# Splitting K into its two fp16 halves on POOL from an fp32 copy, and ACT's projection copy between a slot's two exponentials

## The chip, the cores and the metric

One core of a Trainium2 chip runs the whole kernel in one launch. The engines that matter are PE (TensorE, matrix products), ACT (ScalarE), DVE (VectorE), POOL (GpSimd) and SP (SyncE), which here only issues transfers. The metric is the device time of one execution in microseconds (us).

## The reference, cut to what matters

Four transformer-like layers run over `x` of 16 batches x 56 tokens x 128 features. Layers 1, 2 and 3 each hold a cross-attention over the same context `ctx`, 16 x 1500 x 128, with 16 heads of 8 features:

```
h   = (ctx - mean) / sqrt(var + eps)          # layers 1 and 2 (layer 1 scales and shifts it too); layer 3 uses ctx as it is
k   = h @ Wk + bk ;  v = h @ Wv + bv          # 1500 x 128 each, per batch
att = softmax(q @ k.T / sqrt(8))              # 56 x 1500 per head
x   = x + (att @ v) @ Wo + bo
```

Layer 0 is one attention over `ctx` with a mixture of three experts behind it; layers 2 and 3 also have a self-attention over 56 tokens ahead of the cross-attention and a feed-forward block behind it. All is fp32 in the reference. The kernel forms `q @ k.T` from fp16 halves: k_hi is k rounded to fp16 and k_lo = k - k_hi, again in fp16; q is treated likewise, and the products hi·hi, hi·lo and lo·hi are summed in one matrix product over 50 rows.

## The kernel before, in words

Every engine has its own instruction stream, written out by hand, and the streams meet through semaphores (`wait_ge` on one, `then_inc` to another). An engine executes its stream strictly in order, so a wait holds back all that stands behind it.

A cross-attention (`cross`, once per layer 1, 2 and 3) is a software pipeline over 16 batches, `pipeline`: `attend(batch, following, behind, third)` works on batch b, on b+1 (`following`), b+2 (`behind`) and b+3 (`third`) at once. One attend is cut into 12 slots c, each for 125 context rows. In slot c, PE computes the scores of b (`scores`, 8 products into two halves, L1153), then two or three `unit` products of b+1 (L1101), whose maximum DVE takes (L1552), in odd slots the products of probabilities and v of two earlier slots (`values`, L1127), and last one `misc` step. ACT takes the two exponentials of the slot (L795), one for each half of the scores. PE's scores of slot c+1 wait for the first exponential of slot c, so for little else.

The misc steps prepare context for later batches. There are nine for a batch (`MISC`): T0, T1, T2 transpose the context (L1011), K0, K1, K2 form k (L1016, 500 context rows each), V0, V1, V2 form v (L1022). `SLOT_MISC` places them: V2 of b+1 in slot 0; T0, T1, T2, K0 of b+2 in slots 1 to 4; K1, K2 in 6 and 8; V0, V1 in 9 and 10. They all use one PSUM bank, so that a misc product must wait until the one before has been copied out. ACT copies it out (`misc` in ACT's part: T at L717 or L720, K at L725, V at L729) at the start of the next slot, ahead of that slot's exponentials. For a K step, ACT writes k_hi (fp16) and DVE then reads the bank again and k_hi, and writes k_lo (L1460, `k_low`); PE's next misc product waits for both (L1000, L1001). On DVE `k_low` stands behind the maxima of the slot. Before the pipeline of a layer starts, the misc steps of batches 0 and 1 run beside the expert network of layer 0 or beside the self-attention (`ahead`).

SP moves k on: `k_out` (L407) writes the two halves of a third of k to DRAM, `k_in` (L419) reads it back in six pieces so that the heads lie as the matrix products need them. It waits for `k_lo_done` and for the transfers before it. In one attend SP issues k_out 0, k_in 0, k_out 1, k_in 1, k_out 2 for b+2, and then `load` (L373): the context of b+4, 750 KB, into one of two buffers. The third k_in of that batch comes at the start of the next attend.

POOL normalises the context of b+3 (`normalise`, 12 instructions at L585) in layers 1 and 2, once it has been loaded; in layer 3 it does nothing in the pipeline. In the self-attention POOL copies operands for each of the 16 batches (`self_copies`, L544 to L548). The ring of probabilities has RING = 6 slots.

## Time and profile before

| | |
|---|---|
| median of 3 runs | 2066.11 us (2053.47 to 2067.04) |
| the profiled execution | 2056.51 us, span of its instructions 2054.7 us |
| mean granted TensorE clock | 0.892 of full speed |
| busy share of the span | PE 80%, DVE 60%, ACT 49%, POOL 21% |

The profile is of one execution. PE's share is a modelled one, since its products are pipelined. In a timeline, a row gives the start (us from the span's start), the duration, engine, line, operation, output and input with shapes, the number of instructions merged, and in square brackets the idle time of the engine just before it with what ended it. "issue" there means that the profile shows nothing that was waited for. "SPq" is the issue of a transfer on SP; its duration is that of the issue and not of the transfer. The cross-attentions lie at about 410 to 800 us (layer 1), 1005 to 1410 us (layer 2) and 1610 to 2010 us (layer 3).

### The profile page before, as it was taken

The page shows a single profiled execution, that of the slowest core. Times are in us where ns is not written, and L with a number is a line of the kernel's source. Part 1 is how long each engine was busy: PE and PEld are TensorE (multiplying, and loading weights), DVE is VectorE, ACT ScalarE, POOL GpSimd, SP SyncE. Part 2 cuts the span into 40 slices and gives each one's busy share as a digit, 9 for nine tenths or more (in the row PEclk, how much of TensorE's full clock was granted, in tenths as well). Part 3 has the DMA queues.
Part 4 walks back from the last instruction along what each step waited for, and adds up shares of the span by engine and source line. Part 5 has one row for each costly group of instructions (what it writes and reads, how often), then busy time and mean ns, then how long its engine had stood idle before and what let it go on. Part 6 is the DMA issues. An engine that isn't in the chain of part 4 may idle for free.

```text
span 2054.7 us, 53923 instructions
## 1 busy us (share of the span) xinstructions
PE 1635.4 (80%) x20495; PEld 1030.7 (50%) x20495; DVE 1236.0 (60%) x2433; ACT 1004.1 (49%) x1911; POOL 422.9 (21%) x611
## 2 busy tenths in 40 slices
PE   4788777588887887787688888887785888888876
PEld 3465544255555555443355555555342455555554
DVE  5454443567775776364677777773364777777762
ACT  1243322166665666242366666663242466666662
POOL 7000133013331333135033333310131000000000
PEclk9798988599998998796699999996796799999997
DMA  5021122234443442040344444430040444444410
GB/s 174 26 77 64 45 44 62 55 82 112 112 110 94 113 102 73 1 103 3 72 112 113 111 109 111 110 98 14 0 102 11 92 116 117 114 114 112 106 43 9
DMA packets 178537, 166.32 MB, mean 81 GB/s; under 512 B 67551, under 2 KB 168098, under 8 KB 178402
## 3 DMA queue, kind: packets, MB, share of 16 engines
q1 hardware_dynamic: 176818, 163.35, 30.2%
q8 instruction: 97, 1.59, 0.4%
q10 hardware_dynamic: 1008, 1.05, 0.2%
q14 instruction: 38, 0.31, 0.0%
q0 software_dynamic: 576, 0.02, 0.0%
HBM read 114.46 MB, written 40.08 MB: 75 GB/s over the span
## 4 chain that ended last, share of the span: by engine, by line
PE 64%; issue 13%; DVE 10%; ACT 10%; DMA 1%; POOL 1%; ACTq 0%; DVEq 0%; SPq 0%; POOLq 0%
PE PS L1127 11%; PE PS L1022 8%; PE PS L1153 8%; PE PS L1016 8%; PE PS L862 6%; PE PS L1101 5%; PE PS L1011 3%; PE PS L941 3%; ACT q_parts L795 2%; DVE mx L1552 2%; PE PS L1227 2%; PE PS L959 2%; ACT v_sb L729 2%; ACT cxT L720 2%; PE PS L932 1%
## 5 line engine op out<-in xcount | busy, mean ns | idle before, releaser
L1552 DVE TENSOR_REDUCE mx<-PS 112x1 f32<-112x500 f32 x1152 | 718.4, 671 | 295.8 <-PE PS L1101 291.5
L795 ACT ACTIVATE q_parts<-PS 125x448 f32<-125x448 f32 x1152 | 562.2, 544 | 108.8 <-PE PS L1153 105.0
L585 POOL TENSOR_SCALAR cx<-cx,norm_b 125x128 f32<-125x128 f32 x384 | 303.5, 813 | 590.7 <-DMA cx<-in_ctx 488.2
L1153 PE MATMUL PS<-q_st,k_st 50*125 50x112 f16 x4608 | 263.1, 236 | 40.1 <-ACT q_parts L795 23.2
L1153 PEld LDWEIGHTS PS<-q_st,k_st 50*125 50x125 f16 x4608 | 186.4, 140 | 213.7 <-ACT q_parts L795 121.7
L1101 PE MATMUL PS<-k_st,q_mx 50*112 50x500 f16 x1152 | 262.5, 403 | 38.8 <-issue 24.2
L1127 PE MATMUL PS<-q_parts,v_sb 125*18 125x112 f32 x9216 | 291.4, 270 | 0.0
L1127 PEld LDWEIGHTS PS<-q_parts,v_sb 125*18 125x18 f32 x9216 | 218.4, 101 | 60.7 <-issue 52.1
L729 ACT ACTIVATE v_sb<-PS 125x512 f32<-125x512 f32 x144 | 87.1, 605 | 186.7 <-PE PS L1022 186.6
L725 ACT ACTIVATE k_hi<-PS,vec 128x500 f16<-128x500 f32 x144 | 97.5, 677 | 129.0 <-PE PS L1016 129.0
L1101 PEld LDWEIGHTS PS<-k_st,q_mx 50*112 50x112 f16 x1152 | 91.5, 133 | 74.5 <-issue 44.9
L1460 DVE SCALAR_TENSOR_TENSOR k_lo<-PS,vec,k_hi 128x500 f16<-128x500 f32 x144 | 104.8, 728 | 20.0 <-ACT k_hi L725 20.0
L1011 PE MATMUL PS<-ident,cx 125*128 125x125 f32 x576 | 97.1, 293 | 22.6 <-ACT cxT L717 11.8
L1011 PEld LDWEIGHTS PS<-ident,cx 125*128 125x128 f32 x576 | 62.6, 146 | 63.4 <-issue 26.3
L1022 PE MATMUL PS<-L_xcond_Wkv,cxT 128*125 128x128 f32 x384 | 61.1, 308 | 27.3 <-issue 22.6
L1022 PE MATMUL PS<-L_xcond_W_kvc,cxT 128*125 128x128 f32 x384 | 61.1, 308 | 25.0 <-issue 22.9
L1016 PE MATMUL PS<-cxT,L_xcond_Wkv 128*128 128x500 f32 x96 | 54.7, 653 | 30.8 <-issue 25.9
L813 ACT ACTIVATE A<-A 56x896 f32<-56x896 f32 x32 | 30.4, 949 | 92.4 <-DVE A L1661 92.4
L1022 PE MATMUL PS<-L_xcond_ca_vw,cxT 128*125 128x128 f32 x384 | 55.2, 287 | 25.3 <-issue 22.9
L782 ACT ACTIVATE q_st<-PS 2x448 f16<-2x448 f32 x48 | 25.7, 535 | 101.4 <-PE PS L1112 100.0
L1392 DVE TENSOR_REDUCE neg<-PS 56x1 f32<-56x1500 f32 x16 | 27.4, 1711 | 77.1 <-PE PS L941 77.1
L1022 PEld LDWEIGHTS PS<-L_xcond_Wkv,cxT 128*125 128x125 f32 x384 | 52.2, 209 | 42.2 <-issue 36.5
(266 smaller groups left out, 1994.1 us busy)
## 6 DMA issues: line engine op xcount, KB each, us to landing
k_st<-k_dram SPq DMA_DIRECT2D x864, 62.5 KB, 2.2
cx<-in_ctx SPq DMA_DIRECT2D x56, 750.0 KB
k_dram<-k_hi SPq DMA_DIRECT2D x144, 125.0 KB, 1.8
k_dram<-k_lo SPq DMA_DIRECT2D x144, 125.0 KB, 2.0
v_sb<-in_ctx SPq DMA_DIRECT2D x8, 750.0 KB
q_mx<-q_all SPq DMA_DIRECT2D x48, 99.8 KB
q_st<-q_all SPq DMA_DIRECT2D x48, 99.8 KB
q_all<-q_dram SPq DMA_DIRECT2D x18, 196.0 KB, 6.4
```

The source lines that it names most:

```text
L585: last = pool.tensor_scalar(cx[:, p, c, :], cx[:, p, c, :], norm_b[:, p, 0, c:c + 1], norm_b[:, p, 1, c:c + 1], ALU.subtract, ALU.mult)
L729: act.activation(v_sb[:, p, TC * t:TC * t + TC, :, 0:2 * DH], PS[0:KC, bank, :].rearrange("p (c r d) -> p c r d", c=TC, r=NP), ACT.Copy)\
L795: act.activation(probs[:, c % RING, u * HR:(u + 1) * HR], PS[0:KC, (2 * c + u) % SC_RING, 0:HR], ACT.Exp).then_inc(sem("exp_done"), 1)
L862: last = mm(dst[:, u, :], wt, r(u), start=(k == 0), stop=(k == len(rows) - 1))
L1011: last = pe.transpose(PS[:, bank, c * KC:(c + 1) * KC], cx[:, p, TC * t + c, :], ident[0:KC, 0:KC])
L1016: mm(PS[:, bank, 0:TK], cr["kw"], cxT[:, TK * t:TK * t + TK], start=True, stop=True)\
L1022: last = mm(PS[0:KC, bank, c * D:(c + 1) * D], cxT[:, k0:k0 + KC], cr["vw"], start=True, stop=True)
L1101: mm(PS[0:PW, MX_BANK + u % MX_RING, 0:TK], q_mx[64 * a:64 * a + ROWS, p, k, :], k_st[64 * a:64 * a + ROWS, p, k, TK * t:TK * t + TK], sta ...
L1127: last = mm(PS[32 * j:32 * j + VW, PV_BANK, k * PW:k * PW + PW], v_sb[:, p, c, r, :], probs[:, c % RING, r * PW:r * PW + PW], start=(c == ...
L1153: last = mm(PS[0:KC, (2 * c + a) % SC_RING, k * PW:k * PW + PW], k_st[64 * a:64 * a + ROWS, p, k, c * KC:(c + 1) * KC], q_st[64 * a:64 * a ...
L1460: dve.scalar_tensor_tensor(out=k_lo[:, cols], in0=PS[:, bank, 0:TK], scalar=cr["kb"], in1=k_hi[:, cols], op0=ALU.add, op1=ALU.subtract)\
L1552: dve.tensor_reduce(mx[:, r, t:t + 1], PS[0:PW, MX_BANK + u % MX_RING, 0:TK], AX.X, ALU.max)\
```

## The change

ACT now writes a K step out of PSUM as fp32, with its bias, into a new tile `k_full`, which has two buffers by the parity of the batch. POOL makes both halves from it: `split_keys` rounds a third of it to k_hi (a copy, 128 x 500) and subtracts (k_lo = k_full - k_hi, 128 x 500). DVE's `k_low` is gone everywhere, and PE's next misc product waits for `k_full_done` alone. On POOL the three splits of `behind` stand in each attend, behind `normalise(third)`; the splits of batches 0 and 1 (`split_first`) stand ahead of a layer's pipeline, which in layers 2 and 3 is behind all of `self_copies`. In a cross-attention's slot, ACT now does the first exponential, then the copy of the misc product of the slot before, then the second exponential. RING is 4 instead of 6, which makes room for `k_full`.

```diff
-RING = 6
+RING = 4
...
+        k_full = sb("k_full", [128, 2, S])
...
+            def split_keys(layer, batch, t):
+
+                b, i, p = batch
+                n = B * (layer - 1) + b
+                cols = slice(TK * t, TK * t + TK)
+                ge_known(pool, ("k_full_done", NT * n + t + 1), (f"k_out{t}", 32 * n))
+                pool.tensor_copy(k_hi[:, cols], k_full[:, p, cols]).then_inc(sem("k_hi_done"), 1)
+                ge_known(pool, ("k_hi_done", NT * n + t + 1))
+                pool.tensor_tensor(k_lo[:, cols], k_full[:, p, cols], k_hi[:, cols], ALU.subtract)\
+                    .then_inc(sem("k_lo_done"), 1)
+
+            def split_first(layer):
+                for b in range(2):
+                    for t in range(NT):
+                        split_keys(layer, (b, 0, b), t)
...
                     if third and cr["norm"] is not None:
                         copies(third)
                         normalise(third)
+                    if behind:
+                        for t in range(NT):
+                            split_keys(layer, behind, t)
...
                 self_copies(2)
+                split_first(2)
                 cross_copies(2, True)
...
-                        ge(act, f"k_out{t}", 32 * n)
-                        act.activation(k_hi[:, TK * t:TK * t + TK], PS[:, bank, 0:TK], ACT.Identity, bias=cr["kb"])\
-                           .then_inc(sem("k_hi_done"), 1)
+                        ge(act, "k_lo_done", NT * (n - 2) + t + 1)
+                        act.activation(k_full[:, p, TK * t:TK * t + TK], PS[:, bank, 0:TK], ACT.Identity, bias=cr["kb"])\
+                           .then_inc(sem("k_full_done"), 1)
...
-                        if k is not None and (following if of_next else behind):
-                            misc(following if of_next else behind, k)
                         ge(act, "pv_done", n - (RING - 1))
                         for u in range(2):
                             act.wait_ge(sem("scores_ready"), 2 * n + u + 1)
                             act.activation(probs[:, c % RING, u * HR:(u + 1) * HR],
                                            PS[0:KC, (2 * c + u) % SC_RING, 0:HR], ACT.Exp).then_inc(sem("exp_done"), 1)
+                            if u == 0 and k is not None and (following if of_next else behind):
+                                misc(following if of_next else behind, k)
...
                         if was == "K":
-                            pe.wait_ge(sem("k_hi_done"), NT * n + wt + 1)
-                            pe.wait_ge(sem("k_lo_done"), NT * n + wt + 1)
+                            pe.wait_ge(sem("k_full_done"), NT * n + wt + 1)
...
-                    dve.wait_ge(sem("k_hi_done"), NT * n + t + 1)
-                    ge(dve, f"k_out{t}", 32 * n)
-                    cols = slice(TK * t, TK * t + TK)
-                    dve.scalar_tensor_tensor(out=k_lo[:, cols], in0=PS[:, bank, 0:TK], scalar=cr["kb"],
-                                             in1=k_hi[:, cols], op0=ALU.add, op1=ALU.subtract)\
-                       .then_inc(sem("k_lo_done"), 1)
```

First place: POOL in the repeated body of layer 1's pipeline, from one attend's normalising to the next one's, before (cx is the context, norm_b and mod_b hold a batch's factors):

```order
L585 TENSOR_SCALAR cx<-cx,norm_b 125x128 x12
L569 ISA
L569 COPY norm_b<-mean_all 125x12
L571 REGISTER_ALU
L571 COPY norm_b<-rstd_all 125x12
L222 REGISTER_ALU
L577 ISA
L577 COPY mod_b<-mod 128x2
L278 ISA
L585 TENSOR_SCALAR cx<-cx,norm_b 125x128 x12
```

The same place in the change, as far as the second split (the lines have shifted):

```order
L602 TENSOR_SCALAR cx<-cx,norm_b 125x128 x12
L279 ISA
L567 CAST k_hi<-k_full 128x500
L569 TENSOR_TENSOR k_lo<-k_full,k_hi 128x500
L279 REGISTER_ALU
L567 CAST k_hi<-k_full 128x500
```

Behind the twelve instructions that normalise b+3 stand now the pairs that split the keys of b+2, three of them; before, the next attend's copies followed at once.

Second place: ACT in the first slots of layer 1's first attend, with what each row waits for, before:

```order
L795 ACTIVATE q_parts<-PS 125x448 [waits scores_ready] x2
L729 ACTIVATE v_sb<-PS 125x32x16 [waits v_ready]
L795 ACTIVATE q_parts<-PS 125x448 [waits scores_ready] x2
L717 ACTIVATE cxT<-PS,mod_b 128x500 [waits mod_copied,cxT_ready]
L795 ACTIVATE q_parts<-PS 125x448 [waits scores_ready] x2
L717 ACTIVATE cxT<-PS,mod_b 128x500 [waits cxT_ready]
```

and in the change:

```order
L816 ACTIVATE q_parts<-PS 125x448 [waits scores_ready] x3
L752 ACTIVATE v_sb<-PS 125x32x16 [waits v_ready]
L816 ACTIVATE q_parts<-PS 125x448 [waits scores_ready] x2
L740 ACTIVATE cxT<-PS,mod_b 128x500 [waits mod_copied,cxT_ready]
L816 ACTIVATE q_parts<-PS 125x448 [waits scores_ready] x2
L740 ACTIVATE cxT<-PS,mod_b 128x500 [waits cxT_ready]
```

Each copy out of the misc bank (v_sb, cxT) has moved behind one more exponential (q_parts), the first of its slot.

## Rows read from the trace of the kernel before

**Rows 1.** Timeline of DVE and PE, layer 2, around one batch's K steps

```profile
1202.93 0.73 DVE L1460 SCALAR_TENSOR_TENSOR k_lo<-PS,vec,k_hi 128x500 f16<-128x500 f32 x1
...
1203.76 1.08 PE L1016 MATMUL PS<-cxT,L_xcond_W_kvc 128*128 128x500 f32 x2 [0.57 <-issue]
...
1208.05 1.08 PE L1016 MATMUL PS<-cxT,L_xcond_W_kvc 128*128 128x500 f32 x2 [0.86 <-issue]
...
1212.33 1.11 PE L1022 MATMUL PS<-L_xcond_W_kvc,cxT 128*125 128x128 f32 x8 [1.53 <-issue]
```

**Rows 2.** Timeline of SP's transfer issues, layer 2, one load to the next

```profile
1215.23 0.31 SPq L373 DMA_DIRECT2D cx<-in_ctx  x1
...
1228.82 0.34 SPq L407 DMA_DIRECT2D k_dram<-k_hi  x1
...
1240.32 0.31 SPq L373 DMA_DIRECT2D cx<-in_ctx  x1
```

**Rows 3.** Timeline of POOL: normalising batches 4 and 15 (layers 1, 2) and between

```profile
447.02 9.35 POOL L585 TENSOR_SCALAR cx<-cx,norm_b 125x128 f32<-125x128 f32 x12 [27.37 <-issue]
...
746.62 9.35 POOL L585 TENSOR_SCALAR cx<-cx,norm_b 125x128 f32<-125x128 f32 x12 [17.48 <-DMA cx<-in_ctx]
...
939.39 9.35 POOL L585 TENSOR_SCALAR cx<-cx,norm_b 125x128 f32<-125x128 f32 x12 [0.20 <-POOL norm_b L571]
...
1043.48 9.35 POOL L585 TENSOR_SCALAR cx<-cx,norm_b 125x128 f32<-125x128 f32 x12 [84.30 <-DMA cx<-in_ctx]
...
1225.83 9.35 POOL L585 TENSOR_SCALAR cx<-cx,norm_b 125x128 f32<-125x128 f32 x12 [18.40 <-DMA cx<-in_ctx]
...
1331.49 9.35 POOL L585 TENSOR_SCALAR cx<-cx,norm_b 125x128 f32<-125x128 f32 x12 [17.84 <-DMA cx<-in_ctx]
```

**Rows 4.** POOL's groups of instructions: busy us, mean ns of one

```profile
L585 POOL TENSOR_SCALAR cx<-cx,norm_b 125x128 f32<-125x128 f32 x384 | 303.5, 813 | 590.7 <-DMA cx<-in_ctx 488.2 <-issue 102.0 <-POOL norm_b L571 0.4
L548 POOL TENSOR_TENSOR q_parts<-A,mask 128x896 f32<-128x896 f32 x32 | 54.1, 1689 | 0.0
...
L545 POOL COPY A_first<-A 128x112 f32 x28 | 7.9, 282 | 0.0
L544 POOL COPY A_first<-A 128x56 f32 x28 | 6.5, 231 | 95.5 <-PE PS L1227 95.5
```

**Rows 5.** Timeline of PE and ACT, layer 2, slot 1

```profile
1219.56 0.43 PE L1153 MATMUL PS<-q_st,k_st 50*125 50x112 f16 x8
1219.67 0.61 ACT L729 ACTIVATE v_sb<-PS 125x512 f32<-125x512 f32 x1 [0.51 <-PE PS L1022]
...
1220.17 0.97 ACT L795 ACTIVATE q_parts<-PS 125x448 f32<-125x448 f32 x2
1220.41 0.64 PE L1011 MATMUL PS<-ident,cx 125*128 125x125 f32 x4 [0.20 <-ACT v_sb L729]
```

**Rows 6.** Timeline of ACT, layer 2, the next batch's first K copy

```profile
1226.32 0.68 ACT L725 ACTIVATE k_hi<-PS,vec 128x500 f16<-128x500 f32 x1 [0.41 <-PE PS L1016]
```

**Rows 7.** Ends of the self-attention of layer 3: POOL's last copy, SP's next issue

```profile
1555.44 1.69 POOL L548 TENSOR_TENSOR q_parts<-A,mask 128x896 f32<-128x896 f32 x1
...
1584.04 0.81 SPq L441 DMA_DIRECT2D q_dram<-q_parts  x2
```

**Rows 8.** Stretches of layer 1: busy time of each engine, then PEclk

```profile
625.00:630.00 5.00, 1.82 (x12) 1.31 (x13) 0.77 (x2) 0.98 (x2) 0.00 (x0) 0.66 0.38 126
...
635.00:640.00 5.00, 5.00 (x56) 3.33 (x54) 2.53 (x4) 2.98 (x6) 5.00 (x9) 0.50 0.00 0
```

**Rows 9.** Timeline of PE, layer 1, scores of slots 2 and 4, twice

```profile
634.52 0.67 PE L1153 MATMUL PS<-q_st,k_st 50*125 50x112 f16 x8
...
640.24 0.44 PE L1153 MATMUL PS<-q_st,k_st 50*125 50x112 f16 x8
...
663.43 0.44 PE L1153 MATMUL PS<-q_st,k_st 50*125 50x112 f16 x8
...
667.06 0.44 PE L1153 MATMUL PS<-q_st,k_st 50*125 50x112 f16 x8
```

More of the change, by code:

```diff
@@ L616, in _ @@
                     pool.memset(v_sb[:, p, :, :, 2 * DH:VW], 1.0).then_inc(sem("v_ones"), 1)
+                split_first(1)
                 cross_copies(1, True)
@@ L623, in _ @@
                 self_copies(3)
+                split_first(3)
                 cross_copies(3, True)
@@ L1444, in l0_last @@
                 l0_evidence(b)
-            def preparation(layer):
-                cr = cross_of(layer)
-                n0 = B * cr["n"]
-                def k_low(batch, k, bank=MISC_BANK):
-                    kind, t = MISC[k]
-                    if kind != "K":
-                        return
-                    b, i, p = batch
-                    n = n0 + b
-                    dve.wait_ge(sem("k_hi_done"), NT * n + t + 1)
-                    ge(dve, f"k_out{t}", 32 * n)
-                    cols = slice(TK * t, TK * t + TK)
-                    dve.scalar_tensor_tensor(out=k_lo[:, cols], in0=PS[:, bank, 0:TK], scalar=cr["kb"],
-                                             in1=k_hi[:, cols], op0=ALU.add, op1=ALU.subtract)\
-                       .then_inc(sem("k_lo_done"), 1)
-                return k_low
             l0_batches(l0_first, l0_both, l0_last, dve)
@@ L1471, in _ @@
             dve.tensor_copy(halves(A[5]), pair(0)).then_inc(sem("evid_done"), 1)
-            k_low = preparation(1)
             for e in range(E):
@@ L1493, in _ @@
             for k in range(2 * E + 1):
-                if layers > 1:
-                    ahead(k_low, AHEAD[3 * k:3 * k + 1], DENSE_BANK)
                 dve.wait_ge(sem("hid_tanh"), k + 1)
@@ L1502, in _ @@
                                          op0=ALU.add, op1=ALU.mult).then_inc(sem("hid_done"), 1)
-                if layers > 1:
-                    ahead(k_low, AHEAD[3 * k + 1:3 * k + 3], DENSE_BANK)
                 if k == 1:
@@ L1544, in cross @@
                     last.then_inc(sem("q_split"), 1)
-                k_low = preparation(layer)
                 def unit(batch, u):
@@ L1616, in attend @@
                             unit(following, t)
-                        of_next, k = SLOT_MISC.get(c - 1, (True, None))
-                        if behind and not of_next:
-                            k_low(behind, k)
                     if following:
@@ L1641, in self_attention @@
                 s, _, bs, _, ob = SELF[layer]
-                k_low = preparation(layer)
                 dve.wait_ge(sem("self_lin"), 2 * s + 1)
@@ L1675, in both @@
                     front(n)
-                    ahead(k_low, beside[0:1], SELF_BANK)
                     back(b)
-                    ahead(k_low, beside[1:3], SELF_BANK)
                 batches(dve, front, both, back)
```

## The prediction

> **What bounds the kernel now.** I read the page first: PE is 80% busy, so any gain has to show as less idle time of PE. In a batch's timeline PE stands still before K1, before K2 and before V0, for 0.57, 0.86 and 1.53 us, always until just after DVE's k_lo (the one shown ends at 1203.66, K1 starts at 1203.76) [rows 1]. That is 2.96 us a batch of a period of about 26. Next I read what else runs in a circle. SP's issues show that from the first k_out of a batch to the next load of context pass 11.5 us (1228.82 to 1240.32) [rows 2], nearly all of it spent on issuing and on landings in between, not on waiting for keys. POOL's rows show that the load issued at 1215.23 releases its normalising at 1225.83, 10.6 us later [rows 2, 3], and that this takes 9.35 us, most of it while POOL would otherwise be idle [rows 3]. So POOL, at 21%, looks free; the question is when.
>
> **The step that decides: where POOL's splits stand.** POOL's stream is in order, and the splits of b+2 stand behind the normalising of b+3. In the batch shown ACT copies K0 out at 1226.32, while POOL has begun to normalise at 1225.83 and goes on until 1235.18 [rows 3, 6]. Before, k_lo did not care; now it must wait. And what waits for k_lo on SP is k_out 0, with the load of b+4 five steps behind it on the same queue, and that load is what POOL's next normalising waits for. That closes a ring which was open:
>
> - load to the start of normalising: 10.6 us [rows 2, 3]
> - normalising: 9.35 us [rows 3]
> - a wait on POOL's own semaphore, 0.20 as after its copies of norm_b [rows 3], then the copy of 128x500: the two copies of 56 and 112 columns took 231 and 282 ns, so 0.91 ns a column and 231 + 444 x 0.91 = 635 ns [rows 4]; 0.20 again; the subtraction by the row with two inputs, 1689 ns for 896 columns, so 1.88 x 500 = 0.94 us [rows 4]. Together 2.0 us.
> - SP notices, 0.1 us as between k_lo and K1 on PE [rows 1]; k_out 0 to the next load 11.5 us [rows 2]
>
> The sum is 33.5 us a batch. The buffers do not give way: each load needs the k_out of the attend before. The second and third split (1.8 us each) come before SP gets to them and cost nothing.
>
> The ring turns eleven times in a layer, from the load of batch 4 to that of 15. Before, those eleven took 746.62 - 447.02 = 299.6 us in layer 1 (a disturbance near 625 included) and 1331.49 - 1043.48 = 288.0 us in layer 2 [rows 3]. At 33.5 they take 368.5: **+68.9 and +80.5, together +149 us**. Both ends line up as before: at the first turn the delay is absorbed, at the last the keys of 14 are ready about when attend 13 starts.
>
> The bounds of POOL's price: the lowest slope is the copies' 0.91 ns a column for the subtraction too, 0.5 us less a turn; the highest is that of normalising, 813 ns for 128 columns [rows 4], 3.2 us for each, 4.9 us more a turn, so -11 and +108 us over 22 turns. I take the middle rows, because plain copies and a plain tensor-tensor operation are what is added. The load could take 9 us when nothing else moves, or 12: +-33 us.
>
> The Trainium skill (GPSIMD Engine Reference, section 4.1) speaks against this move for another reason: elementwise work with two inputs belongs on VectorE, GpSimd being about half as fast. The rows agree: 1.6 us for the pair on POOL against 0.73 on DVE [rows 1, 4]. Priced by that rule alone the move would lose under 1 us of an idle engine for each K step, which is nothing on the path, and the sum would be some 150 us lower. It is the place in the queue that costs here, not the speed.
>
> **The other steps.** *PE's wait on k_lo falls away*: -2.96 us a batch [rows 1]. *The copy between the two exponentials* gives some of it back and more. In slot 1 the scores start at 1219.56, ACT copies V2 out at 1219.67 and T0 starts at 1220.41, 0.85 us after the scores [rows 5]. Now that copy has to wait for the scores (0.43), start and run the first exponential (0.03 and the pitch of 0.97 - 0.54 = 0.43), then copy (0.61) and tell PE (0.13, from 1220.28 to 1220.41): 1.63 us after the scores, so +0.78. Slots 2, 4 and 10 are built alike, with no `values` to cover it: +0.85 each. In slots 3 and 9 `values` covers all but 0.1. In slot 11 the second exponential and the shift behind it are later, +0.2. The sum is 3.6 us, against 2.96 saved: **+0.7 us a batch**, where PE sets the pace. What the new order should spare, PE's scores waiting for an exponential behind a copy, is not seen as idle PE time in these rows. Layer 3 has no normalising and so no ring: 14 batches, +10 us. In layers 1 and 2 about four batches each run outside the ring: +6.
>
> *DVE's k_lo gone beside the dense part and the self-attentions*: 18 K steps, each worth between 0 and 0.86 us [rows 1]; I take 0.6, -11 us.
>
> *`split_first` behind all of self_copies*: in layer 3 POOL's last copy ends at 1557.1, while SP starts to move q at 1584.04 [rows 7]. In between SP must now move two batches of keys, each 11.5 us and a third k_in, about 4: 1557.1 + 2.0 + 31 = 1590, **+6 us**. In layer 2 a layer norm stands in between and hides it, and in layer 1 the keys are made long before; if these were not hidden, they would cost 6 each. *RING = 4*: PE does `values` for slot c-3 before the scores of slot c+1, so the ring never holds 5 slots: nothing. If it did bind, it would be by one `values`, under 1 us a slot.
>
> **Sum**: 149 + 10 + 6 - 11 + 6 = +160 us on the profiled 2056.5, giving 2217. The median of the three runs lies 0.5% above that execution, part of which a slower kernel shares; I forecast 2218.
>
> **Rivals.**
> 1. *No ring, PE sets the pace, the exponentials' order bites.* POOL would have to be through with normalising when K0 comes; the row at 1225.83 against 1226.32 speaks against it [rows 3, 6]. 42 batches x 0.7 = +29, -11, +6: 2081. 7%.
> 2. *No ring and the order does not bite* (ACT would find the second half's scores no earlier anyway): -2.96 x 42 = -124, -11, +6: **faster, 1928**. It decides if POOL splits K0 within a slot or two of ACT's copy. For it speaks the plain PE wait in rows 1, against it the same rows as above. 7%.
> 3. *The ring, and PE falls to half clock in it.* PE would wait several us in each attend. Layer 1 shows what follows: PE was busy 1.82 of 5 us at 625 to 630, and the granted clock of 635 to 640 is 0.50, the 1.2 GHz level, with PE busy all the time [rows 8]. Slots 2 and 3 then took 5.72 us (634.52 to 640.24) against 3.63 at full clock (663.43 to 667.06), 1.58 times as long [rows 9]. An attend of 25.8 us at that level throughout would be 40.7, more than the ring's 33.5, and PE would bound: 22 x 7.2 = +158, 2376. But by 663 the scores of PE run at full clock again [rows 9], so only part of each attend would be slow; with a third of it at the low level an attend takes 25.8 + 0.33 x 14.9 = 31 and still fits. Half of it mixed in would be 2297. 8% for clearly above 2280. The Trainium skill (TensorE: Matmul & The Clock Gate, Part 1) says that the throttled state is the default and activity releases it, which is why I expect PE to win its clock back within each attend rather than stay low; by the rule alone PE would not bound and the sum stands.
> 4. *The forecast*: 78%.
>
> **Range and chances.** The forecast's own bounds: POOL's price and the load, -44 to +60 with the far row of POOL discounted, and layer 3 from -41 (order does not bite) to +20. Few of these add up, so 2165 to 2285 takes in four fifths. A change under 1%, about 21 us, is what a measurement of this kernel cannot tell from none. Rival 1 lies just beyond it, at its edge: 0.03 same, 0.07 faster, 0.90 slower.
>
> **What would show it.** POOL's CAST of K0 starts within 0.5 us of the last normalising instruction in layers 1 and 2, not of ACT's copy; loads in these layers are 33.5 us apart and in layer 3 about 26; L585 still waits for the load. PE's idle time gathers before `unit` or the scores at the start of an attend, 6 to 8 us, as "issue" or on a transfer of k_st. In layer 3 K1, K2 and V0 start without a wait for keys, while T0, T1, K0 and V1 wait for ACT 0.8 us each, and the batch takes 0.7 us longer. The CAST takes about 0.64 us and the subtraction 0.94. Wrong would be: loads 26 us apart in layer 2 (rivals 1, 2), PE without idle time at clock 0.5 (rival 3), or layer 3 shorter by 40 us.

## The result, and the profile after

| | before | after |
|---|---|---|
| median | 2062.36 us (2053.47 to 2067.04, 4 runs) | 2249.15 us (2232.30 to 2264.22, 4 runs) |
| ratio to before, 95% interval | 1 | **1.0909** (1.0821 to 1.0997) |
| the profiled execution, its span | 2056.51, 2054.7 | 2232.30, 2230.5 |
| granted TensorE clock | 0.892 | 0.836 |

The change makes the kernel 9.1% slower. The forecast was 2218 us and its range, 2165 to 2285, holds the result. One execution of e5 and one of e7 below were over 1.5% above the fastest of their kernel, at a lower clock; e7's ratio leaves its one out, while e5's counts it and would be about 1.116 without it. Engines in the page of the changed kernel (busy us, share of the span, instructions), and its chain of waits:

```profile
PE 1737.2 (78%) x20495; PEld 1094.7 (49%) x20495; DVE 1162.4 (52%) x2289; ACT 1005.5 (45%) x1911; POOL 675.5 (30%) x899
...
PE 49%; POOL 11%; DMA 10%; ACT 9%; DVE 9%; issue 7%; SPq 5%; ACTq 0%; POOLq 0%; DVEq 0%
```

POOL, off the path before (1% of the chain), now makes up 11% of it, and DMA 10%. PE is busy for 1737.2 us where it was 1635.4, with the same 20495 instructions: the same products ran at a lower clock. In layer 3 that is a second loss beside the ring, and the prediction left it out there.

**The ring, as [rows 2, 3, 6] now read.** POOL in layer 2 of the changed kernel, with the first and the last normalising of the eleven turns around two consecutive ones:

```profile
1104.42 9.36 POOL L602 TENSOR_SCALAR cx<-cx,norm_b 125x128 f32<-125x128 f32 x12 [15.83 <-DMA cx<-in_ctx]
...
1238.86 9.36 POOL L602 TENSOR_SCALAR cx<-cx,norm_b 125x128 f32<-125x128 f32 x12 [18.38 <-DMA cx<-in_ctx]
1248.17 0.60 POOL L567 CAST k_hi<-k_full 128x500 f16<-128x500 f32 x1
1248.92 1.13 POOL L569 TENSOR_TENSOR k_lo<-k_full,k_hi 128x500 f16<-128x500 f32 x1 [0.15 <-POOL k_hi L567]
...
1272.35 9.36 POOL L602 TENSOR_SCALAR cx<-cx,norm_b 125x128 f32<-125x128 f32 x12 [18.37 <-DMA cx<-in_ctx]
1281.66 0.60 POOL L567 CAST k_hi<-k_full 128x500 f16<-128x500 f32 x1
...
1472.87 9.36 POOL L602 TENSOR_SCALAR cx<-cx,norm_b 125x128 f32<-125x128 f32 x12 [19.01 <-DMA cx<-in_ctx]
```

SP's issues between the two, and ACT's copy of K0 that belongs to the split at 1281.66:

```profile
1250.14 0.34 SPq L408 DMA_DIRECT2D k_dram<-k_hi  x1
...
1261.55 0.31 SPq L374 DMA_DIRECT2D cx<-in_ctx  x1
```

```profile
1269.90 0.67 ACT L748 ACTIVATE k_full<-PS,vec 128x500 f32<-128x500 f32 x1
```

Read it as a circle: normalising starts at 1238.86, its last instruction ends when the CAST starts (1248.17), the subtraction ends at 1250.05, SP issues k_out 0 at 1250.14 and the load at 1261.55, and that load releases the next normalising at 1272.35. The legs are 11.28, 11.41 and 10.80 us, together 33.49. From 1104.42 to 1472.87 eleven turns take 368.45 us, 33.50 each. K0 lay ready in k_full from 1270.57 on, and POOL came to it 11.1 us later. In [rows 6] ACT's copy began 0.5 us after the normalising. Here it ended 1.8 us before it, while POOL had nothing in hand: the normalising stands next in POOL's stream and waited for its load, and the split stands behind both. Over the 24 normalisings of b+3 in layers 1 and 2, ACT's copy of K0 begins between 4.3 us before and 2.7 us after POOL's normalising, and each time the CAST follows the last normalising instruction at once.

**Prices, the answer to [rows 4]** (POOL's groups: busy us, mean ns of one | idle before):

```profile
L602 POOL TENSOR_SCALAR cx<-cx,norm_b 125x128 f32<-125x128 f32 x384 | 306.8, 814 | 469.2 <-DMA cx<-in_ctx 448.4 <-issue 20.8
L569 POOL TENSOR_TENSOR k_lo<-k_full,k_hi 128x500 f16<-128x500 f32 x144 | 164.3, 1141 | 21.0 <-POOL k_hi L567 3.6
L567 POOL CAST k_hi<-k_full 128x500 f16<-128x500 f32 x144 | 87.7, 609 | 539.9 <-ACT k_full L748 320.4 <-issue 219.5
```

The mean of a CAST came out at 0.61 us (forecast 0.64), that of the subtraction at 1.14 (forecast 0.94).

**What answers to [rows 1, 5], in layer 3.** Timeline at full clock: K0, K1 and V0 on PE in one attend, then slot 1 of the next attend on PE and ACT:

```profile
2047.78 1.11 PE L1038 MATMUL PS<-cxT,L_xcond_ca_kw 128*128 128x500 f32 x2 [0.90 <-ACT cxT L743]
...
2050.87 1.10 PE L1038 MATMUL PS<-cxT,L_xcond_ca_kw 128*128 128x500 f32 x2
...
2056.97 1.14 PE L1044 MATMUL PS<-L_xcond_ca_vw,cxT 128*125 128x128 f32 x8
...
2066.17 0.43 PE L1175 MATMUL PS<-q_st,k_st 50*125 50x112 f16 x8
...
2066.64 0.55 ACT L816 ACTIVATE q_parts<-PS 125x448 f32<-125x448 f32 x1 [0.94 <-PE PS L1175]
2067.08 0.60 ACT L752 ACTIVATE v_sb<-PS 125x512 f32<-125x512 f32 x1
...
2067.73 0.65 PE L1033 MATMUL PS<-ident,cx 125*128 125x125 f32 x4 [0.91 <-ACT v_sb L752]
```

K1 (2050.87) and V0 (2056.97) start without a wait, where [rows 1] had 0.57 and 1.53 us. T0 starts 1.56 us after its slot's scores, where [rows 5] had 0.85 and the prediction 1.63: the copy now stands behind an exponential that waits for those scores. Over 360 us of layer 3 before and 380 us after (what PE waited for: us in total, times, longest), first before:

```profile
PE PS L1022 <- issue: 21.4, 14, 1.5
PE PS L1016 <- issue: 20.0, 28, 0.9
```

```profile
PE PS L1044 <- ACT v_sb L752: 13.0, 14, 1.0
PE PS L1033 <- ACT cxT L743: 12.6, 14, 1.0
PE PS L1038 <- ACT cxT L743: 12.6, 14, 1.0
PE PS L1033 <- ACT v_sb L752: 12.4, 13, 1.0
```

The rows that say "issue" are the waits on k_lo of [rows 1]. So 41.4 us of waits on k_lo have turned into 50.6 us of waits on ACT, in 14 batches each. These are 0.9 us at each of four steps of a batch: T0, T1, K0 and V1.

**What answers to [rows 7].** The end of the self-attention of layer 3, first POOL's last copy and first split, then SP's last load and the move of q:

```profile
1696.05 1.69 POOL L549 TENSOR_TENSOR q_parts<-A,mask 128x896 f32<-128x896 f32 x1
1697.68 0.60 POOL L567 CAST k_hi<-k_full 128x500 f16<-128x500 f32 x1
...
1721.97 8.94 SPq L420 DMA_DIRECT2D k_st<-k_dram  x18
1731.09 0.81 SPq L442 DMA_DIRECT2D q_dram<-q_parts  x2
```

SP moves q (1731.09) as soon as the keys of batch 1 are issued.

### The profile page after: what moved, and what is told of

Its sections match the earlier page's. It is cut to its first block, busy times and chain, and to the rows that moved or that the text cites. A ratio compares the mean times of both kernels' runs of the same rounds, so it can differ in the third digit from the quotient of the medians.

```text
span 2230.5 us, 54153 instructions
## 1 busy us (share of the span) xinstructions
PE 1737.2 (78%) x20495; PEld 1094.7 (49%) x20495; DVE 1162.4 (52%) x2289; ACT 1005.5 (45%) x1911; POOL 675.5 (30%) x899
## 4 chain that ended last, share of the span: by engine, by line
PE 49%; POOL 11%; DMA 10%; ACT 9%; DVE 9%; issue 7%; SPq 5%; ACTq 0%; POOLq 0%; DVEq 0%
POOL cx L602 9%; PE PS L1175 7%; PE PS L1149 6%; PE PS L1044 5%; PE PS L885 5%; PE PS L1038 4%; PE PS L1033 4%; DMA cx<-in_ctx 4%; SPq L420 4%; PE PS L1123 3%; DMA k_st<-k_dram 3%; PE PS L964 2%; DMA k_dram<-k_lo 2%; DVE mx L1547 2%; ACT q_parts L816 2%
## 5 line engine op out<-in xcount | busy, mean ns | idle before, releaser
L816 ACT ACTIVATE q_parts<-PS 125x448 f32<-125x448 f32 x1152 | 603.6, 544 | 601.5 <-PE PS L1175 593.8
L1123 PE MATMUL PS<-k_st,q_mx 50*112 50x500 f16 x1152 | 286.0, 444 | 127.8 <-DMA k_st<-k_dram 73.2
L1149 PE MATMUL PS<-q_parts,v_sb 125*18 125x112 f32 x9216 | 322.1, 286 | 2.6
L1175 PE MATMUL PS<-q_st,k_st 50*125 50x112 f16 x4608 | 281.9, 249 | 36.4 <-ACT q_parts L816 23.5
L567 POOL CAST k_hi<-k_full 128x500 f16<-128x500 f32 x144 | 87.7, 609 | 539.9 <-ACT k_full L748 320.4
L1033 PE MATMUL PS<-ident,cx 125*128 125x125 f32 x576 | 124.5, 355 | 82.8 <-ACT v_sb L752 37.7
L569 POOL TENSOR_TENSOR k_lo<-k_full,k_hi 128x500 f16<-128x500 f32 x144 | 164.3, 1141 | 21.0 <-POOL k_hi L567 3.6
L1033 PEld LDWEIGHTS PS<-ident,cx 125*128 125x128 f32 x576 | 80.7, 179 | 136.6 <-issue 49.4
L748 ACT ACTIVATE k_full<-PS,vec 128x500 f32<-128x500 f32 x144 | 96.8, 672 | 16.1 <-PE PS L1038 16.1
L1249 PE MATMUL PS<-q_parts,A_first 128*56 128x448 f32 x128 | 71.3, 646 | 0.0
```

The source lines that it names most:

```text
L569: pool.tensor_tensor(k_lo[:, cols], k_full[:, p, cols], k_hi[:, cols], ALU.subtract)\
L748: act.activation(k_full[:, p, TK * t:TK * t + TK], PS[:, bank, 0:TK], ACT.Identity, bias=cr["kb"])\
L816: act.activation(probs[:, c % RING, u * HR:(u + 1) * HR], PS[0:KC, (2 * c + u) % SC_RING, 0:HR], ACT.Exp).then_inc(sem("exp_done"), 1)
L1033: last = pe.transpose(PS[:, bank, c * KC:(c + 1) * KC], cx[:, p, TC * t + c, :], ident[0:KC, 0:KC])
L1123: mm(PS[0:PW, MX_BANK + u % MX_RING, 0:TK], q_mx[64 * a:64 * a + ROWS, p, k, :], k_st[64 * a:64 * a + ROWS, p, k, TK * t:TK * t + TK], sta ...
L1149: last = mm(PS[32 * j:32 * j + VW, PV_BANK, k * PW:k * PW + PW], v_sb[:, p, c, r, :], probs[:, c % RING, r * PW:r * PW + PW], start=(c == ...
```

## The experiments

The experiments were timed in three groups, each beside the kernel before, and each ratio, with its 95% interval, is to the kernel before in the same group. Between groups there is more than these intervals show: one and the same kernel, e6, gave 0.9477 in one group and 0.9614 in another. The first four change one thing in the changed kernel; e5 adds two parts of the change, the copy's place and RING = 4, to the kernel before.

**e1: the splits ahead of the normalising.**

```diff
-                    if third and cr["norm"] is not None:
-                        copies(third)
-                        normalise(third)
                     if behind:
                         for t in range(NT):
                             split_keys(layer, behind, t)
+                    if third and cr["norm"] is not None:
+                        copies(third)
+                        normalise(third)
```

> POOL splits the keys of b+2 ahead of normalising b+3 in each attend, everything else as in the change. Ring theory (the splits' place behind the normalising closes a ring of 33.5 us through SP's load): that ring opens, but a shorter one closes, T0 of a batch to K2 (about 17.6 us), split 1.9, normalising 9.6, T0 of the next batch: about 29 us a batch in layers 1 and 2, so 22 x 4.3 = 95 us less than the change, 2135 us in the profile, ratio to before 1.04. Speed theory (POOL is slower than DVE at the split, wherever it stands): no change, ratio 1.09.

Measured: 2176.75 us, 1.0602 (1.0533 to 1.0671). Loads are about 30.8 us apart in layer 2, so the ring opened by 2.7 us a turn where 4.3 was expected, and the ratio stands above the 1.04 expected. In 360 us of that layer T0 waits for POOL's cx eleven times, 25.2 us together. POOL now waits for ACT's copy of K2 before it may normalise, and so is late with the context of b+3.

**e2: normalising in three pieces between the splits.**

```diff
-                        normalise(third)
-                    if behind:
-                        for t in range(NT):
-                            split_keys(layer, behind, t)
+                    for t in range(NT):
+                        if behind:
+                            split_keys(layer, behind, t)
+                        if third and cr["norm"] is not None:
+                            normalise(third, t)
```

> POOL takes split 0, a third of the normalising, split 1, a third, split 2, a third. The same instructions on POOL as in the change. Ring theory: no ring is left that is longer than PE's own pace; the loads lie 26 to 27 us apart in layers 1 and 2, the kernel is within 2% of before, ratio 1.00 to 1.02 (above 1 because the copy between the exponentials costs 0.7 us a batch more than k_lo's wait gave). Speed theory: ratio 1.09.

Measured: 2126.30 us, 1.0332 (1.0284 to 1.0379), loads 28.5 apart on average in layer 1 and 27.9 in layer 2. The speed theory falls, but the ring theory's 1.00 to 1.02 was missed too: the loads stayed 1 to 2 us above its 26 to 27, and layer 3's cross-attention, 448.8 us, is 27 above the kernel before. `normalise(third, t)` does the four instructions of one third. PE's waits on keys are gone in 360 us of layer 2; 41.6 us of waits on ACT's copies are left there.

**e3: the load of b+4 ahead of the three k_out on SP.**

```diff
                         q_max(behind)
+                        if not (isinstance(b, int) and b + 4 >= B):
+                            load((b + 4, i + 2, p))
                         k_out(behind, 0)
...
                         k_out(behind, 2)
-                        if not (isinstance(b, int) and b + 4 >= B):
-                            load((b + 4, i + 2, p))
```

> SP issues the load of b+4 ahead of k_out 0 instead of behind k_out 2; POOL is left as in the change, with the splits behind the normalising. Ring theory: the load no longer waits for keys, so the ring opens at SP instead of at POOL: loads 26 to 28 us apart in layers 1 and 2, ratio 1.00 to 1.03. If it is POOL's order alone that costs, by holding the keys back whatever SP does, the ratio stays above 1.06.

Measured: 2122.19 us, 1.0304 (1.0258 to 1.0350), at the upper end of what was expected. Loads are 27.1 apart on average in layer 2 and 29.7 in layer 1 (one of them 39.4). POOL's order is untouched here and the splits still stand behind the normalising; only SP's leg is off the circle. PE's waits on keys are gone in 360 us of layer 2. That two edits on two different engines give back the same 5 to 6% of the time shows the circle, rather than either place, to be the cause.

**e4: ACT's copy back ahead of both exponentials.**

```diff
+                        if k is not None and (following if of_next else behind):
+                            misc(following if of_next else behind, k)
                         ge(act, "pv_done", n - (RING - 1))
...
-                            if u == 0 and k is not None and (following if of_next else behind):
-                                misc(following if of_next else behind, k)
```

> The change, but with ACT's copy of the projection back ahead of the slot's first exponential. Slot theory (the copy between the exponentials costs PE about 3.6 us a batch in slots 1, 2, 4, 10 and 11 wherever PE sets the pace): layers 1 and 2 stay at 33.5 us a batch since the ring sets it there; layer 3 becomes 14 x 3.6 = 50 us shorter and the ends of layers 1 and 2 some 20 us, ratio to before about 1.06. Rival (the new order is neutral): ratio 1.09.

Measured: 2189.86 us, 1.0644 (1.0593 to 1.0695). Layers 1 and 2 do not move: loads stay 33.3 us apart, and PE waits longer for keys instead of waiting for ACT. In layer 2, about the same eleven batches, after (first line) and e4 (second):

```profile
PE PS L1123 <- DMA k_st<-k_dram: 39.3, 13, 5.3
```

```profile
PE PS L1123 <- DMA k_st<-k_dram: 69.8, 20, 6.4
```

So the two losses lie side by side in layers 1 and 2, and the longer one counts. All of e4's gain is in the cross-attention of layer 3, 392.3 us against 444.0 in the changed kernel; those of layers 1 and 2 differ by under 1 us from it. Against the kernel before, layer 3 of e4 shows the worth of the k_lo wait alone. Batches from K0 to K0 at full clock (length, PE busy, granted clock, DMA share, GB/s), before and then e4:

```profile
1824.99:1851.15 26.16, 22.53 (x370) 1.00 0.44 118
1851.15:1876.24 25.09, 21.41 (x362) 1.00 0.42 110
```

```profile
1943.50:1965.60 22.10, 21.34 (x362) 1.00 0.49 124
1965.60:1990.07 24.47, 22.56 (x370) 1.00 0.47 124
```

A batch of 362 products falls from 25.09 to 22.10, by 2.99 us, which is the 2.96 of [rows 1]. The other kind, which has the closing products of a pair too, gives only 1.7, so that the mean is 2.3. Two of 13 successive batches of e4's layer 3 show a clock below 1.00 as well, 0.93 and 0.87; in each PE first waited once for keys, 2.4 and 1.9 us.

**e5: the order alone.** The kernel before with the copy between the exponentials and RING = 4; ACT still writes k_hi and DVE k_lo.

```diff
-RING = 6
+RING = 4
...
-                        if k is not None and (following if of_next else behind):
-                            misc(following if of_next else behind, k)
...
+                            if u == 0 and k is not None and (following if of_next else behind):
+                                misc(following if of_next else behind, k)
```

> The kernel before, with two parts of the change alone: ACT's copy of a misc product stands between a slot's two exponentials, and RING is 4. ACT still writes k_hi, DVE still writes k_lo, POOL does not split. There is no ring through POOL here, so PE sets the pace in all three layers. Theory (the order costs PE about 0.8 us at each of T0, T1, K0 and V1, and the waits on k_lo stay): a plain batch of layer 3 takes about 25.1 + 5.0 = 30.1 us from K0 to K0, or 28.7 by the 3.6 us of the prediction; over 42 batches +150 to +210 us, 1.07 to 1.10 of the kernel before. Rival (the order costs nothing by itself, and what is seen in layer 3 of the changed kernel comes from the splits): 25.1 us a batch, ratio 1.00. Second rival (k_lo's wait hides the copy's delay in part, since the two do not add): 27 us a batch, 1.03 to 1.04.

Measured: 2316.71 us, **1.1224** (1.1121 to 1.1327), worse than the whole change. Two batches of its layer 3 (columns as above):

```profile
1947.63:1976.36 28.73, 21.65 (x363) 1.00 0.39 101
...
2063.92:2095.10 31.18, 24.36 (x363) 0.89 0.36 93
```

At full clock the order costs 28.73 - 25.09 = 3.64 us, the 3.6 of the prediction; in batches of the other kind (29.45, 29.42) it is 3.3. The second row is the same work with the clock lowered for a part of it: 2.45 us more. Of 13 successive batches of layer 3, seven show 0.89 or less, two 0.94 and only four 1.00, while all 13 were at 1.00 before. The 13 took 5.5 us a batch more than before, which over 42 batches would be 1.11; so the clock is what lifts the ratio above the theory. RING = 4 did not bind: in 200 us of layer 3 ACT's exponentials wait 87.0 us for PE's scores and never for `values`. Both rivals, that the order is free and that it hides behind k_lo's wait, fall.

**e6: e2 and e4 together,** both diffs as above.

> The changed kernel with two edits: POOL normalises b+3 in three pieces of four instructions (3.1 us each) between the splits of b+2, and ACT copies a misc product out ahead of the slot's first exponential, as before the change. Theory (the ring through POOL and the order on ACT are the two losses, and each goes with its own edit; the saving on k_lo stays): the ring turns in 28 us or less in layers 1 and 2, layer 3 runs at the 22.1 and 24.5 us a batch that the copy set back gave alone (loads 23.7 apart); against the kernel before: layer 3 -22 us, layers 1 and 2 still held by the ring at about 28 to 28.5 (22 x 2 = +44), dense and self -10, split_first +12: ratio 1.01 of the kernel before. Rival (the ring's 28 us of the interleaved kernel were set by PE's waits on ACT, not by POOL): the loads of layers 1 and 2 close to 24 to 25 us apart too and the ratio is 0.96 to 0.97.

Measured: 1964.84 us, **0.9477** (0.9409 to 0.9544); once more in another group, as e6_again, 1975.81, 0.9614 (0.9569 to 0.9659). The theory's 1.01 fell and the rival won, in one group with more than its 0.96 to 0.97: loads are 23.8 us apart on average in layer 2, against 26.2 before, and mostly 23 to 26 in layer 1, with three of 29.5 to 34.4. So e2's 28 us were set by PE's waits on ACT, not by POOL. What POOL does in layer 2 of it:

```profile
1174.70 0.60 POOL L567 CAST k_hi<-k_full 128x500 f16<-128x500 f32 x1 [7.49 <-issue]
...
1176.61 3.12 POOL L603 TENSOR_SCALAR cx<-cx,norm_b 125x128 f32<-125x128 f32 x4
1179.68 0.60 POOL L567 CAST k_hi<-k_full 128x500 f16<-128x500 f32 x1
```

The split no longer stands behind 9.36 us of normalising, and the pieces seldom wait for their load.

**e7: e3 and e4 together,** both diffs as above.

> The changed kernel with two edits: SP issues the load of b+4 ahead of the three k_out of b+2 instead of behind them, and ACT's copy stands ahead of the slot's exponentials, as before the change. With the load early, SP's part of the ring (k_out 0 to the load, 11.5 us) is off it: what is left is load to normalising 10.6, normalising 9.35, splits 5.6, and a k_out before the next round, which is below 27 us. Theory (with both off, PE sets the pace): 24 to 25 us from load to load in all three layers, ratio 0.96 to 0.97 of the kernel before. Rival (the attend's end that frees the buffer, or the keys that come back late from DRAM, still bind at 28): ratio 1.01.

Measured: 1988.38 us, 0.9563 (0.9479 to 0.9647), loads 25.1 apart on average in layer 2. The theory held: with the circle open and the order back, the time falls below that of the kernel before. PE still waits there for keys, 14.9 us in 360.

**e8: a longer turn.**

```diff
+        spare = sb("spare", [128, 2000], F16)
...
+                if t == 0:
+                    pool.memset(spare[:, :], 0.0).then_inc(sem("k_ones"), 1)
+                    ge_known(pool, ("k_ones", n + 4))
                 pool.tensor_copy(k_hi[:, cols], k_full[:, p, cols]).then_inc(sem("k_hi_done"), 1)
```

POOL's rows of it in layer 2:

```profile
1264.74 1.76 POOL L569 MEMSET spare<- 128x2000 f16 x1
1266.64 0.60 POOL L571 CAST k_hi<-k_full 128x500 f16<-128x500 f32 x1
```

> The changed kernel, and POOL fills a spare tile of 128 x 2000 fp16 ahead of each batch's first split: some 1.8 to 2.0 us more of POOL between the last normalising instruction and the split of K0, in every batch. Nothing reads the tile. Theory (that split closes the ring of layers 1 and 2): loads are 33.5 + 2.0 = 35.5 us apart in layers 1 and 2, 22 turns x 1.95 = +43 us on the changed kernel, 1.11 of the kernel before; in layer 3, where POOL has time to spare, loads stay 26.9 apart. Rival (POOL's splits are beside the path and the 33.5 us come from something else): the time of the changed kernel, 1.09.

Measured: 2315.21 us, 1.1170 (1.1089 to 1.1250). The split moves by 1.90 us (1264.74 to 1266.64). The eleven turns take 35.35 and 35.53 us each in layers 1 and 2, where the changed kernel's take 33.40 and 33.50; loads of layer 3 are 27.0 apart, against 26.9. So the added work is paid in full, turn by turn, in the two layers with normalising and not in the third, which puts the split on the circle. 22 turns account for 44 us; by the ratios the kernel is 54 us slower than the changed one, and the intervals alone leave some 25 us either way. In the profiled executions the difference is 86 us: 44 of them are the turns, 31 lie outside the turns in the cross-attentions of layers 1 and 2, and 11 in that of layer 3; these 42 were not followed up.

**e9: e6 and the early load; e10: e6 with the first keys split inside the self-attention; e11: both.**

```diff
-                copies((0, 0, 0))
-                copies((1, 0, 1))
-                with pool.Fori(1, B // 2) as i:
+                for b in range(10):
+                    copies((b, b // 2, b % 2))
+                    if b in (4, 9):
+                        for t in range(NT):
+                            split_keys(layer, (b // 5, 0, b // 5), t)
+                with pool.Fori(5, B // 2) as i:
...
                 self_copies(3)
-                split_first(3)
```

> The changed kernel with three edits: POOL's normalising of b+3 in three pieces between the splits of b+2, SP's load of b+4 ahead of the three k_out, and ACT's copy ahead of the slot's exponentials. With either of the first two, loads of layers 1 and 2 were already 23 to 25 us apart, about what layer 3 takes, so PE sets the pace and a third edit has little left to win. Theory: within 1% of the interleaved kernel with the copy set back, 0.94 to 0.955 of the kernel before. Rival (the ring still binds now and then, in the batches of 25 to 30 us that remain): 0.93.

> The interleaved kernel with the copy set back, and POOL splits the keys of batches 0 and 1 inside the self-attention (batch 0 behind its fifth set of copies, batch 1 behind its tenth) instead of behind all 16. Theory (the 11.8 us by which the stretch from the self-attention of layer 3 to its cross-attention grew come from SP, which cannot move q before those keys): that stretch falls from 31.7 back to about 20 us, and the time by 10 to 12 us, 0.5 to 0.6%. In layer 2 nothing changes, a layer norm hides it. Rival (q's way through DRAM was late for another reason): the same time as without the edit.

> All four edits on the changed kernel: normalising in pieces between the splits, the load ahead of the k_out, the copy ahead of the exponentials, and the first two batches' keys split inside the self-attention. Theory: 10 to 12 us less than with the first three, 0.935 to 0.95 of the kernel before. Rival: no further gain, because PE sets the pace from end to end.

> The interleaved kernel with the copy set back once more, on the same chip as the three kernels that are built on it, since 10 us are to be told apart: 0.948 of the kernel before, as it was.

| kernel | median us | ratio | interval |
|---|---|---|---|
| e6_again | 1975.81 | 0.9614 | 0.9569 to 0.9659 |
| e9 | 1990.49 | 0.9695 | 0.9655 to 0.9734 |
| e10 | **1946.24** | **0.9470** | 0.9423 to 0.9516 |
| e11 | 1979.75 | 0.9646 | 0.9605 to 0.9686 |

e9 stands 0.8% above e6_again. That is within the 1% expected, but a loss where a gain was the rival, and both kernels lie above the ratios that were expected of them (0.94 to 0.955 and 0.948). The early load costs: layer 2's cross-attention takes 411.2 and 411.8 us in e9 and e11, and 398.1 to 399.6 in e10, e6 and e6_again, which lack it. In layer 2 its loads are 25.1 us apart on average instead of 23.7, and in 360 us of that layer PE waits 16.5 us for keys instead of 8.4. SP's rows show where e9 is late, e9 first, then e6_again:

```profile
1177.23 0.46 SPq L374 DMA_DIRECT2D cx<-in_ctx  x1
1177.91 0.35 SPq L408 DMA_DIRECT2D k_dram<-k_hi  x1
...
1186.36 2.67 SPq L420 DMA_DIRECT2D k_st<-k_dram  x6
```

```profile
1155.39 0.34 SPq L408 DMA_DIRECT2D k_dram<-k_hi  x1
...
1158.52 2.67 SPq L420 DMA_DIRECT2D k_st<-k_dram  x6
```

From k_out 0 to the first issue of the k_in that waits for it pass 8.45 us behind a load of 750 KB, and 3.13 us without one just ahead. By the Trainium skill (DMA: Bandwidth & Descriptors, Queues, rings and completion order) descriptors of one ring are taken in the order in which they were put there. The rows fit it, but transfers that share the engines would look alike, and no run tells the two apart.

PE at the end of layer 3's self-attention in e10, from its output projection to the first product of the cross-attention:

```profile
1489.38 3.36 PE L889 MATMUL PS<-A,L_xcond_sa_ow 128*128 128x448 f32 x4 [1.59 <-DVE A L1675]
...
1509.43 1.05 PE L1127 MATMUL PS<-k_st,q_mx 50*112 50x500 f16 x3 [12.12 <-issue]
```

That is 20.05 us; in the changed kernel it is 31.69 (1713.34 to 1745.03) and before 19.91. So the 11.8 us asked about are back. The median of e10 lies 30 us under e6_again's, more than the 10 to 12 expected. In the profiled executions e10 is 24.1 us shorter, of which 12.0 are this stretch and 11.3 the cross-attention of layer 1, which the edit does not touch; what caused that is open. e11 against e9 gives 11 us, as expected, though its ratio lies above the 0.935 to 0.95 expected. e10 is the fastest kernel here, 5.3% under the kernel before; some 12 us of its lead on e6_again are shown.

## Why the prediction was right, and where it was off

Stretches between the same marks of PE in the two profiled executions, before and after (us). The profiled execution after is the fastest of its four, so +175.8 is 11 less than the difference of the medians.

| stretch | before | after | measured | predicted |
|---|---|---|---|---|
| layer 1's cross-attention | 441.8 | 516.3 | +74.5 | +68.9 and 3 of the 6 |
| layer 2's | 433.2 | 517.8 | +84.6 | +80.5 and 3 of the 6 |
| layer 3's | 422.0 | 444.0 | +22.0 | +10 |
| self-attention to cross-attention, layer 3 | 19.9 | 31.7 | +11.8 | +6 |
| ahead of layer 1; the self-attentions | | | -14.6, -2.1, -5.5 | -11 |
| the rest | | | +5.1 | 0 |
| sum | | | +175.8 | +160 |

The total is nearer than some of its parts: layer 3, `split_first` and the rest came out 23 us above the forecast, and the work beside the dense part and the self-attentions 11 below it. That these set each other off in part is luck.

1. **The ring: right.** 33.5 us forecast, 33.50 measured in layer 2 and 33.40 in layer 1; 368.5 for eleven turns, 368.45 measured in layer 2. e8 shows by dose that the split is on it, e2 and e3 that it opens at either of two places. The agreement to 0.1 us is in part luck, since the legs erred against each other: over the eleven turns of layer 2 POOL's leg is 11.29 us (forecast 11.45), SP's 11.76 (11.5; single turns 11.4 to 12.7) and the load's 10.44 (10.6). In POOL's leg the subtraction took 1.13 us for 0.94 and the wait on POOL's own semaphore 0.15 for 0.20. One sign came out smaller than forecast: PE's wait for keys is 39.3 us in 380 us of layer 2, about 3.5 a batch and not 6 to 8, since waits on ACT and slower products take up the rest of PE's spare time.
2. **The subtraction's price.** It was taken at 1.88 ns a column from [rows 4]; measured are 1141 ns for 500, 2.28 ns a column. The Trainium skill (GPSIMD Engine Reference, section 3.1) puts two-input work at about 2.6 cycles an element at 1.2 GHz, by which it would be an estimated 1.08 us here; the trace lies 5% above that, while for the 896 columns of [rows 4] the same rule would give 1.94 us, above the 1.69 measured. No single slope fits both.
3. **The order of the copies: mechanism right, one cost left out.** At full clock it costs 3.64 us (e5) against 3.6, and the waits on k_lo are worth 2.99 (e4) against 2.96, both in batches of 362 products; in the others it is 3.3 and 1.7. But the prediction priced layer 3 at full clock throughout. Batches of the changed kernel there:

```profile
1776.24:1801.83 25.59, 21.34 (x362) 1.00 0.37 94
1882.36:1910.20 27.84, 23.96 (x370) 0.94 0.44 118
1910.20:1937.27 27.07, 23.00 (x362) 0.94 0.40 105
...
2047.78:2074.10 26.32, 22.48 (x371) 1.00 0.42 112
```

   At clock 1.00 the two kinds take 25.59 and 26.32, +0.5 and +0.2 on before (forecast +0.7); a third batch at 1.00 took 26.86, with 0.96 us of waiting for keys in it. At 0.94 they take 27.07 and 27.84, 1.5 us more. Nine of 13 successive batches are at 0.94 or below; together they are 14 us above the same kinds at full clock, out of the 20.8 us by which the 13 grew. That is what the layer's +22 has beyond the forecast +10; at full clock the forecast would have been a little high. Two us at a time, in the batch of 1937 to 1965 (length, PE busy, granted clock, DMA share, GB/s):

```profile
1956.00:1958.00 2.00, 1.09 (x16) 1.00 0.86 192
1958.00:1960.00 2.00, 1.10 (x13) 0.80 0.56 142
1960.00:1962.00 2.00, 2.00 (x29) 0.50 0.31 130
```

   PE waits twice for ACT, ahead of T0 and of T1 (1957.22 and 1959.35, 0.9 us each), is busy for 2.19 of those 4 us, and then the granted clock is 0.50, the 1.2 GHz level, with PE busy throughout. In eight of the nine slow batches the 0.50 begins behind these two waits; the ninth begins while the clock of the one before is still at 0.50. In the kernel before, none of 13 batches of layer 3 is slow and with the order alone (e5) nine are; in the changed kernel nine are, and with the order set back (e4) two. So the new waits cost their own length and slower products behind them. The mis-sized step is "+0.7 us a batch, where PE sets the pace": it holds only at full clock. Why four batches keep the full clock, with the same two waits, was not settled.
4. **In the ring a low clock is free, and rival 3 did not come about.** PE's products take 102 us longer over the whole kernel, mostly in layers 1 and 2, where the granted clock is 0.83 and 0.82 (470 to 790, 1140 to 1500) against 0.97 and 0.98 before (450 to 770, 1060 to 1350). But there PE has time to spare: loads stay 33.4 to 33.5 apart. So the low clock that rival 3 spoke of came in part, and its price did not.
5. **`split_first`**: right in place, half the measured size, +6 forecast and +11.8 measured. After POOL's last copy SP needs 1731.09 - 1697.68 = 33.4 us for two batches of keys, as forecast (33); but from the first move of q to PE's start it takes another 1745.03 - 1731.09 = 13.9 us, against 1593.52 - 1584.04 = 9.5 before, which makes up 4.4 of the 5.8 us missed. The six transfers of q_all are issued 6.4 us after q_dram there and 2.0 us after it in e10; that q's writes queue behind k_st's transfers fits this but was not tried alone. e10 takes it all back.
6. **K beside the dense part and the self-attentions**: -22 against -11. The term of 0.6 us for each of 18 K steps was too small. In the first 360 us before, PE waited three times ahead of a K product, 5.9 us together and up to 3.0, more than the 0.86 of [rows 1], and twice ahead of V, 3.5 us, for k_lo; after, its waits on k_full are 3.6 us. That is about 6 of the 14.6 us gained there, and the rest was not followed up.
7. **Rivals 1 and 2 were wrong for this kernel, and yet they described what its parts can do.** With the ring opened and the order set back (e6), what is left of the change is worth 4 to 5%. Rival 2 forecast 1928; e6 took 1965 and 1976, and e10, which has the keys of `split_first` moved too, 1946.

## What to carry to other kernels

Before work is moved to an engine that looks idle, find where it will stand in that engine's stream and follow who waits for it until the path closes or ends: here 21% of POOL was in use, and 1.9 us of new work closed a circle of 33.5, most of it waiting for a load, a 9.4 us block and SP's steps. An engine that stands idle is not free for what stands behind its next wait. When two losses share a layer, undo both: of the changed kernel's time each alone gave back 2 to 6%, and two together 12 to 13%. A copy that frees a buffer for the bounding engine belongs ahead of work that itself waits for that engine, and a short wait that is put into a dense stream of products may cost clock as well as its own length.

## What the hardware showed that was not expected

- Behind two waits of 0.9 us, 2 us apart, the granted clock fell from 1.00 to 0.50 in eight of 13 batches of the changed kernel's layer 3 and stayed at 1.00 in four; the slow ones lost about 1.5 us each. In e4 it fell to about 0.50 behind a single wait of 2.4 us and one of 1.9. In the kernel before, with waits such as the 0.57, 0.86 and 1.53 us of [rows 1] some 4 us apart, layer 3 stayed at 1.00 from 1620 to 1980.
- Two writes of 125 KB to DRAM issued just behind a load of 750 KB were through after at most 8.45 us, and without the load just ahead after at most 3.13 (e9, e6_again).
- POOL's subtraction with two inputs (fp32 and fp16 to fp16, 128 x 500) took 1141 ns, its cast (fp32 to fp16, 128 x 500) 609 ns.
- ACT wrote 128 x 500 from PSUM as fp32 in 672 ns and as fp16 in 677: the wider output cost nothing.
